# Order lists with batch 0 ahead, and cross-attention scores on 32 rows

## The chip, the cores and the metric

One core of a Trainium2 chip runs the kernel. The metric is the device time of one execution in microseconds (us). PE is TensorE, DVE is VectorE, ACT is ScalarE, POOL is GpSimd, SP is SyncE. An engine works through its own list of instructions in order, and waits at each for semaphores that other engines raise.

## The reference

Two transformer layers run one after the other on `x` of 2 batches x 512 tokens x 128 channels, 16 heads of 8 channels, with a context of 77 tokens. Layer norm, modulation and gates stand around each block.

```
layer 0:  qkv = mod(ln(x)) @ W_qkv;  x += gate * (softmax(q k^T / sqrt 8) v @ W_proj)   # all 512 tokens
          qc = ln(x) @ W_qc;  x += softmax(qc kc^T / sqrt 8) vc @ W_cproj                # 77 keys
          x += gate * (gelu(mod(ln(x)) @ W_mlp1) @ W_mlp2)
layer 1:  x += gate * (window attention: windows of 64 tokens, shifted by 32)
          x += gate * cross-attention: per query the 16 largest of 77 scores, softmax over them, times v
          x += gate * ((silu(a) * b) @ w_m2),  a, b = halves of mod(ln(x)) @ w_m1
```

## The kernel before

All is in fp32 but the self-attention of layer 0 (three bf16 parts). Tokens lie on partitions in 4 tiles of 128 per batch. PSUM has six rooms: W0 and W1 of two banks, X0, X1, M0, M1 of one. `rooms_in_turns` (L95) runs through the program once and writes down which result takes which room in which turn; `open_room` (L232) makes PE wait until the room's last result was read. Each engine's order is written out by hand in its block.

- Layer 0's self-attention ends at 163 us. It isn't touched.
- Cross-attention of either layer goes in 16 halves `e` (`HALVES`): batch, tile of 128 tokens, 8 of 16 heads. On PE a half has `cross_scores` (L1552: two products of 4 heads x 77 = 308 columns, with the keys in a block-diagonal `kblk` so that all 128 rows are used), `cross_turn` (L1565, eight transposes of the weights) and, every second half, `cross_pv` (L1575) and `pv_turn` (L1536).
- In layer 0 a half is a maximum (L1262) and a subtraction (L1267) on DVE, an exponential (L885) and two copies of turned weights (L919) on ACT.
- In layer 1 ACT copies the scores (L891); DVE finds the first 8 of each head (MAX8, L1281), strikes them out (MATCH_REPLACE8, L1284), finds the next 8 (L1288) and strikes them out (L1291), 32 instructions of 77 columns per half; POOL subtracts the maximum (L721), ACT takes two exponentials (L904, L909) and POOL multiplies them (L725).
- Window attention goes in 8 units (batch, tile). `window_qk` (L1348) and `v` project; `window_maxima` (L1588) has two groups of 32 small products per unit, each reduced by DVE (L1163); the maxima go back as a row by DMA. `window` (L1606) has, per unit, the scores (S), the products with V (V) and the turn (T). Both batches are projected first, then all units follow in the order of `WINDOWS` (L52).
- Order of the blocks: cross-attention of layer 0 for both batches, its MLP for batch 0 and then 1, window attention, cross-attention of layer 1 for both batches, its MLP for batch 0 and then 1. `ARRIVE` (L63) says at which half the projection, layer norm and query of batch 1 come.
- `project` (L1380) and `mlp_out` (L1392) write `out`, `residual` (L1049) adds it to `x`, `ln_stats` (L955), POOL's `rstd` (L607) and `ln_norm` (L971) follow, then `ln_T` (L1331) and ACT's copy to `hT`.

Of the kernel before, what the change touches and what calls it, by code (L numbers as in the profile page):

```python
# [40 lines left out]
G = 4  # L41
# [10 lines left out]
WINDOWS = "S0 S1 V0 S2 V1 T0 S3 V2 T1 S4 V3 T2 S5 V4 T3 oT S6 V5 T4 out S7 T5 lnT qc".split()  # L52
WINDOWS_LATE = {0: ("V6",), 1: ("V7", "T6"), 2: ("T7",)}
# [9 lines left out]
ARRIVE = ({"oT": -1, "out": 1, "lnT": 3, "qc": 5}, {"oT": 2, "out": 3, "lnT": 4, "qc": 5})  # L63
# [30 lines left out]

def rooms_in_turns():  # L95
# [21 lines left out]
    for layer in range(2):  # L117
        if layer == 1:
            for b in range(B):
                if b:  # L120
                    use("M", "lnT", 3, 1)
                for c in range(NQ):
                    use("M", "qkv", 1, b, "q", c)
                    use("X", "qkv", 1, b, "k", c)
                use("M", "qkv", 1, b, "v")
                for i in range(NT):
                    for half in range(2):
                        use("W", "maxw", b, i, half)
                use("M1", "mT", 1, b)
        if layer == 0:  # L130
            for t in range(STEPS):
                j = t - LOOK - 1
                for q in range(NT):
                    if t < HEADS:
                        use("Y", "max", t, q)
                    if q < 2 and 0 <= t - LOOK < UNITS:
                        use("W", "sT", 0, t - LOOK, q)
                    if q == 1 and t % G == 0 and 1 <= t // G <= B * NG:
                        use("Y", "mT", 0, t // G - 1)
                    if q == 2 and j % NT == 0 and 0 <= j < UNITS:  # L140
                        use("M0", "pv", 0, j // NT)
                for item in EARLY.get(t, ()):
                    for kind, key in EARLY_ROOMS[item]:
                        use(kind, *key)
                if j > 0 and j % NT == 0:
                    use("Y", "pvT", 0, j // NT - 1)
                for at, key in ((T_OUT, ("oT", 0, 0)), (T_OUT + 2, ("out", 0, 0)),
                                (T_OUT + 5, ("lnT", 1, 0)), (T_OUT + 7, ("qc", 0, 0))):
                    if t == at:
                        use("Y", *key)  # L150
        else:
            def window(item):
                u = int(item[1]) if item[1:].isdigit() else None
                if u is None:
                    use("X", *{"oT": ("oT", 2, 0), "out": ("out", 3, 0), "lnT": ("lnT", 4, 0), "qc": ("qc", 1, 0)}[item])
                elif item[0] == "S":
                    for half in range(2):
                        use("W", "sT", 1, u, half)
                else:
                    use(*(("M0", "pv") if item[0] == "V" else ("M1", "pvT")), 1, u)  # L160

            for item in WINDOWS:
                window(item)
        for e in range(-1, HALVES + 3):
            if e + 1 < HALVES:
                use("W", "sc", layer, e + 1)
            if layer == 1:
                for item in WINDOWS_LATE.get(e, ()):
                    window(item)
            if 1 <= e <= HALVES:  # L170
                for part in range(2):
                    use("X", "pT", layer, e - 1, part)
            if e % 2 == 0 and 1 <= e // 2 <= B * NT:
                use("M0", "pvc", layer, e // 2 - 1)
            if e % 2 == 0 and e >= 4:
                use("M1", "pvcT", layer, e // 2 - 2)
            for at, room, key in ((ARRIVE[layer]["oT"], "M1", ("oT", 2 * layer, 1)),
                                  (ARRIVE[layer]["out"], "M1", ("out", 3 * layer, 1)),
                                  (ARRIVE[layer]["lnT"], "W" if layer else "M1", ("lnT", 3 * layer + 1, 1)),
                                  (ARRIVE[layer]["qc"], "W" if layer else "M1", ("qc", layer, 1)),  # L180
                                  (11, "M1", ("oT", 2 * layer + 1, 0)), (13, "M1", ("out", 3 * layer + 1, 0)),
                                  (15, "M1", ("lnT", 3 * layer + 2, 0))):
                if e == at:
                    use(room, *key)
            if e > HALVES:
                for c in (0, 1) if e == HALVES + 1 else (2, 3):
                    use("X", "mlp", layer, 0, c)
                    if layer == 1:
                        use("W", "mlpb", 0, c)
        use("M", "oT", 2 * layer + 1, 1)  # L190
        use("M", "out", 3 * layer + 1, 1)
        use("M", "out", 3 * layer + 2, 0)
        use("M", "lnT", 3 * layer + 2, 1)
        for c in range(NC_):
            use("X", "mlp", layer, 1, c)
            if layer == 1:
                use("W", "mlpb", 1, c)
# [1591 lines left out]
```

## Time and profile before

| | |
|---|---|
| median of 3 runs | 461.62 us (460.95 to 465.91) |
| this profiled execution | 460.53 us, of which the span of instructions is 458.7 |
| PE busy | 374.1 us (82%) |
| DVE busy | 297.2 us (65%) |
| ACT busy | 204.3 us (45%) |
| POOL busy | 111.9 us (24%) |
| mean granted clock of PE | 0.851 |

The page's slices, 11.5 us each, in tenths (the clock row is the granted clock of PE, 9 stands for 0.9 or more):

```profile
PE   3999899999989987899888889978574566675985
...
DVE  4648556999897056666338361235989999997342
ACT  1311126666756935666432123332453555653511
POOL 5332304910010011001015100011434544444010
PEclk9965659999999999999999585566877877776999
```

Self-attention of layer 0 fills slices 1 to 14, its cross-attention and MLP 15 to 21, window attention 22 to 27, the top-16 cross-attention 28 to 36, the end 37 to 40.

### The profile page before, as it was taken

How to read it: one execution, taken by the hardware profiler on the slowest of the kernel's cores; microseconds unless marked ns; L12 is line 12 of the kernel's file. 1: busy time of each engine (PE TensorE's matmuls, PEld its weight loads, DVE VectorE, ACT ScalarE, POOL GpSimd, SP SyncE). 2: the span in 40 equal slices, each digit the busy share in tenths (PEclk: the TensorE clock that was granted, in tenths of full speed). 3: DMA queues.
4: the chain of work that ended last, by engine and by line, in shares of the span. 5: the costliest groups of instructions: out<-in, count | busy, mean ns of one | idle time of the engine just before them, and what ended most of it. 6: DMA issues, size and time to landing. Idle time of an engine off the chain costs nothing.

```text
span 458.7 us, 8982 instructions
## 1 busy us (share of the span) xinstructions
PE 374.1 (82%) x3317; PEld 210.5 (46%) x3317; DVE 297.2 (65%) x1279; ACT 204.3 (45%) x303; POOL 111.9 (24%) x130
## 2 busy tenths in 40 slices
PE   3999899999989987899888889978574566675985
PEld 2325412223333155677655567754353344454454
DVE  4648556999897056666338361235989999997342
ACT  1311126666756935666432123332453555653511
POOL 5332304910010011001015100011434544444010
PEclk9965659999999999999999585566877877776999
DMA  7544625110000000000000000000000000000000
GB/s 201 37 157 120 186 59 156 53 55 2 3 1 2 0 1 1 1 2 1 1 1 2 4 1 7 3 3 1 1 1 1 2 2 1 1 1 1 1 24 24
DMA packets 13247, 12.88 MB, mean 28 GB/s; under 512 B 2373, under 2 KB 11681, under 8 KB 13203
## 3 DMA queue, kind: packets, MB, share of 16 engines
q1 hardware_dynamic: 13007, 12.28, 10.3%
q8 instruction: 27, 0.44, 0.4%
q14 instruction: 17, 0.14, 0.1%
q0 software_dynamic: 160, 0.01, 0.0%
q10 hardware_dynamic: 36, 0.01, 0.0%
HBM read 9.41 MB, written 2.63 MB: 26 GB/s over the span
## 4 chain that ended last, share of the span: by engine, by line
PE 57%; DVE 29%; ACT 7%; issue 5%; POOL 1%; DMA 1%; SPq 0%; ACTq 0%; DVEq 0%; POOLq 0%
PE psum L1491 6%; PE psum L1561 5%; PE psum L1529 5%; DVE left L1284 4%; DVE left L1291 4%; PE psum L1514 4%; DVE mx L1210 4%; PE psum L1355 3%; PE psum L1660 3%; DVE top L1281 3%; DVE top L1288 3%; PE psum L1508 3%; PE psum L1485 2%; PE psum L1544 2%; PE psum L1628 2%
## 5 line engine op out<-in xcount | busy, mean ns | idle before, releaser
L1210 DVE TENSOR_REDUCE mx<-psum 128x1 f32<-128x512 f32 x128 | 81.4, 684 | 26.4 <-PE psum L1491 18.0
L803 ACT ACTIVATE big<-psum 128x1024 f32<-128x1024 f32 x64 | 62.5, 1022 | 46.1 <-PE psum L1514 25.2
L607 POOL TENSOR_TENSOR rstd<-vareps,minus_half 128x4 f32<-128x4 f32 x12 | 12.2, 1020 | 178.8 <-DVE vareps L969 178.7
L1561 PE MATMUL psum<-kblk,qf 128*128 128x308 f32 x128 | 46.0, 490 | 1.1 <-DVE qf L1157 0.8
L1572 PE MATMUL psum<-ident,pr 128*77 128x128 f32 x256 | 38.3, 299 | 10.5 <-POOL pr L725 10.5
L1491 PE MATMUL psum<-KS,QS 72*128 72x512 bf16 x112 | 43.0, 417 | 3.0 <-DVE mx L1210 2.3
L1572 PEld LDWEIGHTS psum<-ident,pr 128*77 128x77 f32 x256 | 34.4, 167 | 18.4 <-POOL pr L725 13.9
L725 POOL TENSOR_TENSOR pr<-pr,early 128x616 f32<-128x616 f32 x16 | 23.9, 1493 | 55.8 <-ACT early L909 37.8
L1529 PE MATMUL psum<-big,V 128*9 128x512 f32 x256 | 34.3, 609 | 0.5 <-ACT big L803 0.5
L1584 PE MATMUL psum<-QS,vc 77*9 77x128 f32 x256 | 13.9, 342 | 24.1 <-ACT QS L919 24.0
L1514 PE MATMUL psum<-QS,KS 75*128 75x512 bf16 x112 | 32.8, 379 | 0.4
L1561 PEld LDWEIGHTS psum<-kblk,qf 128*128 128x128 f32 x128 | 26.4, 227 | 11.1 <-issue 4.3
L1491 PEld LDWEIGHTS psum<-KS,QS 72*128 72x128 bf16 x112 | 9.9, 101 | 45.9 <-issue 25.2
L1040 DVE RECIPROCAL rden<-psum 128x16 f32<-128x16 f32 x24 | 6.1, 254 | 34.8 <-PE psum L1544 34.8
L1291 DVE MATCH_REPLACE8 left<-top,left 128x77 f32<-128x77 f32 x128 | 27.0, 234 | 0.0
L1284 DVE MATCH_REPLACE8 left<-top,gates 128x77 f32<-128x77 f32 x128 | 26.9, 230 | 0.0
L1052 DVE TENSOR_TENSOR x<-psum,x 128x512 f32<-128x512 f32 x12 | 8.3, 691 | 25.5 <-PE psum L1388 15.4
L756 ACT ACTIVATE hT<-psum,mod 128x512 f32<-128x512 f32 x10 | 7.8, 776 | 36.5 <-PE psum L1335 36.5
L919 ACT ACTIVATE big<-psum 77x512 f32<-77x512 f32 x32 | 17.1, 586 | 11.3 <-PE psum L1572 11.2
L1281 DVE MAX8 top<-gates 128x8 f32<-128x77 f32 x128 | 19.5, 228 | 3.8 <-ACT gates L891 3.8
L721 POOL TENSOR_TENSOR early<-gates,top 128x616 f32<-128x616 f32 x16 | 19.6, 1225 | 8.6 <-DVE top L1281 8.2
L891 ACT ACTIVATE gates<-psum 128x616 f32<-128x616 f32 x16 | 10.9, 682 | 22.3 <-PE psum L1561 22.2
(202 smaller groups left out, 687.3 us busy)
## 6 DMA issues: line engine op xcount, KB each, us to landing
QS<-scr_q SPq DMA_DIRECT2D x7, 288.0 KB
KS<-scr_k SPq DMA_DIRECT2D x7, 288.0 KB
scr_q<-qp SPq DMA_DIRECT2D x2, 384.0 KB, 2.9
scr_k<-kp SPq DMA_DIRECT2D x2, 384.0 KB, 3.6
gates<-scr_g SPq DMA_DIRECT2D x2, 320.0 KB, 4.1
early<-in_L_xcond_w_ada_dram SPq DMA_DIRECT2D x1, 576.0 KB, 5.1
scr_k<-kp SPq DMA_DIRECT2D x2, 256.0 KB, 4.3
wmlp<-in_L_xcond_W_mlp_dram SPq DMA_DIRECT2D x2, 256.0 KB, 3.2
```

Source lines behind the costliest of these rows:

```text
L721: pool.tensor_tensor(diff[:, k, :].rearrange("p (h s) -> p h s", s=S), sc[:, k, :].rearrange("p (h s) -> p h s", s=S), top[:, k, :, 0:1].b ...
L725: pool.tensor_tensor(pr[:, k, :], pr[:, k, :], taken[:, k, :], ALU.mult).then_inc(s_pr, 1)
L803: freed(act.activation(pT[:, u % 2, 1024 * half:1024 * (half + 1)], ps, ACT.Exp), "sT", 0, u, half)
L1210: freed(dve.tensor_reduce(mx[:, n % 3, at:at + 1], ps, AX_X, ALU.max), "max", t, q)
L1281: dve.max(top[:, k, h, 0:8], row(sc, h)).then_inc(s_top, 1)
L1284: dve.match_replace(out=row(left, h), in_to_replace=top[:, k, h, 0:8], in_values=row(sc, h), imm_value=-BIG).then_inc(s_top, 1)
L1291: ins_ = dve.match_replace(out=row(left, h), in_to_replace=top[:, k, h, 8:16], in_values=row(left, h), imm_value=-BIG)
L1491: filled(pe.matmul(ps, QS[b][0:ROWS, h, q * P:(q + 1) * P], KS[b][0:ROWS, h, :], start=True, stop=True), "max", j, q)
L1514: last = pe.matmul(ps[:, t * N:(t + 1) * N], KS[b][0:ROWS + 3, h, kt * P:(kt + 1) * P], QS[b][0:ROWS + 3, h, :], start=True, stop=True)
L1529: last = pe.matmul(ps[QUAD * hh:QUAD * hh + DV, :], V[:, b, kt, G * g + hh, :], pT[:, j % 2, hh * N:(hh + 1) * N], start=(kt == 0), stop=( ...
L1561: last = pe.matmul(ps[:, 512 * a:512 * a + HH // 2 * S], qf[:, b, i * P:(i + 1) * P], kb[:, c0:c0 + HH // 2 * S], start=True, stop=True)
L1572: last = pe.transpose(ps[0:S, t * P:(t + 1) * P], pr[:, e % 2, S * h:S * (h + 1)], ident[:, :])
```

## The change

The hand-written loops behind layer 0's self-attention become one list of pieces per engine (`pe_order`, `dve_order`, `act_order`). The names of pieces: `sc` scores, `T` turn of weights, `C` product with the context's V, `D` its turn and division, `oT` turn of the attention's output, `outNB` output N of batch B (0 self, 1 cross, 2 MLP in layer 0; 3, 4, 5 in layer 1), `res` its residual, `statNB` and `normNB` the statistics and norm before stage N, `lnT` its transposes and copy to `hT`, `wqk` and `wv` window projections, `max` maxima, `S`, `V`, `W` scores, product and turn of a window unit (0 to 3 are batch 0, 4 to 7 batch 1). Batch 0 now goes ahead: its window projection comes before batch 1's MLP of layer 0, its cross-attention of layer 1 before the last four window units of batch 1, and its last MLP lies within the halves of batch 1.

Besides that:

- Scores of the cross-attention use the 32 rows of their four heads, and each of the two products another row group. In layer 1 they have room W0 alone; the last four window units have W1 alone.
- Window maxima and scores use 32 rows where they used 8 and 9.
- The gated MLP's second product goes two chunks at a time into a room of two banks.
- POOL's order, and where some tiles lie, follow (`kblk` per batch, `wqkF` in `V`, `pcT` of layer 0 in `QS[0]`, a buffer `oraww`).

```diff
+def cross_pieces(e, layer):
+    last = B * NT * 2
+    found = [("sc", layer, e + 1)] if e + 1 < last else []
+    turns = [("T", layer, e - 1)] if 1 <= e <= last else []
+    if e % 2 == 0 and 1 <= e // 2 <= B * NT:
+        turns.append(("C", layer, e // 2 - 1))
+    if layer == 0 and e % 2 == 0 and e >= 4:
+        turns.append(("D", layer, e // 2 - 2))
+    if layer == 1 and e % 2 and e >= 3:
+        turns.append(("D", layer, (e - 3) // 2))
+    return found, turns
+def pe_order():
+    order = []
+    with_cross0 = {-1: "oT01", 1: "out01", 3: "lnT11", 5: "qc01", 11: "oT10", 12: "out10", 14: "lnT20"}
+    mlp0 = {15: (0, 1), 16: (2, 3)}
+    for e in range(-1, HALVES + 3):
+        found, turns = cross_pieces(e, 0)
+        order += found + turns + pieces(with_cross0.get(e, ""))
+        order += [("mlp0", 0, c) for c in mlp0.get(e, ())]
+        if e == 17:
+            order += [("out", 2, 0)]
+    order += pieces("oT11 lnT30 out11") + [("wqk", 0, 0), ("wqk", 0, 1)] + pieces("lnT21")
+    order += [("wqk", 0, 2), ("wqk", 0, 3)] + [("mlp0", 1, c) for c in range(NC_)] + pieces("wv0")
+    order += [("max", 0, i, half) for i in range(NT) for half in range(2)] + pieces("out21 mT0 lnT31")
+    order += [("wqk", 1, c) for c in range(NQ)]
+    order += pieces("wv1 S0 S1 V0 max100 S2 V1 W0 max101 S3 V2 W1 max110 max111 V3 W2 max120 W3 max121 "
+                    "oT20 max130 max131 out30 mT1 lnT40 qc10")
+    ahead = {0: "S4 S5", 1: "V4 S6 V5", 2: "S7 W5 V6", 3: "W6 V7", 4: "oT21", 6: "lnT41", 10: "oT30", 12: "lnT50"}
+    behind = {1: "W4", 3: "W7", 4: "out31", 6: "qc11", 10: "out40", 15: "out50"}
+    for e in range(-1, HALVES + 1):
+        found, turns = cross_pieces(e, 1)
+        order += found + pieces(ahead.get(e, "")) + turns + pieces(behind.get(e, ""))
+        order += [("mlp1", 0, e - 12)] if e in (12, 13) else []
+    order += [("D", 1, B * NT - 1)] + pieces("oT31 out41 lnT51") + [("mlp1", 1, 0), ("mlp1", 1, 1)] + pieces("out51")
+def dve_order():
+    with_cross0 = {1: "res01 stat11", 2: "norm11", 5: "qc01", 13: "res10 stat20", 14: "norm20", 18: "res20 stat30"}
...
+    order += pieces("norm30 res11 stat21 q00 norm21 q01 q02 q03 v0")
+    order += [("max", 0, i, half) for i in range(NT) for half in range(2)] + pieces("res21 stat31 mT0 norm31")
+    order += pieces("q10 q11 q12 q13 v1 max100 W0 max101 W1 max110 max111 W2 max120 W3 max121 max130 max131 "
+                    "res30 stat40 mT1 norm40 qc10")
+    inside = {2: "W5", 3: "W6", 5: "res31 stat41", 11: "res40 stat50", 13: "gate00 gate01"}
+    behind = {1: "W4", 3: "W7", 5: "norm41", 6: "qc11", 11: "norm50", 14: "gate02 gate03", 15: "res50"}
+    for e in range(HALVES):
+        order += [("first8", e)] + pieces(inside.get(e, "")) + [("next8", e)]
+        if e % 2 and e >= 3:
+            order.append(("D", 1, (e - 3) // 2))
+        order += pieces(behind.get(e, ""))
+    order += [("D", 1, B * NT - 1)] + pieces("res41 stat51 norm51 gate10 gate11 gate12 gate13 res51")
+def act_order():
+    with_cross0 = {0: "oT01", 4: "lnT11", 12: "oT10", 15: "lnT20"}
+    mlp0 = {15: (0, 1), 16: (2, 3)}
...
+    order += pieces("S0 S1 V0 S2 V1 S3 V2 V3 oT20 lnT40")
+    ahead = {0: "S4 S5", 1: "V4 S6 V5", 2: "S7 V6", 13: "mlp100 mlp101"}
+    behind = {3: "V7", 4: "oT21", 6: "lnT41", 10: "oT30", 12: "lnT50", 14: "mlp102 mlp103"}
+    for e in range(HALVES + 2):
+        if e < HALVES:
+            order.append(("copy", e))
+        if 0 <= e - 2 < HALVES:
+            order.append(("T", 1, e - 2))
+        order += pieces(ahead.get(e, ""))
+        if 1 <= e <= HALVES:
+            order.append(("diff", e - 1))
+        if e >= 3 and e % 2:
+            order.append(("C", 1, (e - 3) // 2))
+        if 1 <= e <= HALVES:
+            order.append(("left", e - 1))
+        order += pieces(behind.get(e, ""))
...
+        if kind == "sc":
+            use("W" if args[0] == 0 else "W0", *piece)
...
+        elif kind == "S":
+            for half in range(2):
+                use("W" if args[0] < NT else "W1", "sT", 1, args[0], half)
...
                 for a in range(2):
                     c0 = S * (HH * (e % 2) + HH // 2 * a)
-                    last = pe.matmul(ps[:, 512 * a:512 * a + HH // 2 * S], qf[:, b, i * P:(i + 1) * P],
-                                     kb[:, c0:c0 + HH // 2 * S], start=True, stop=True)
+                    r0 = QUAD * (2 * (e % 2) + a)
+                    last = pe.matmul(ps[:, 512 * a:512 * a + HH // 2 * S], qf[r0:r0 + QUAD, b, i * P:(i + 1) * P],
+                                     kb[r0:r0 + QUAD, c0:c0 + HH // 2 * S], start=True, stop=True)
...
+                            last = pe.matmul(ps[w * WIN:(w + 1) * WIN, j, c * WIN:(c + 1) * WIN],
+                                             QF[q0:q0 + QUAD, b, c, t0:t0 + WIN], KF[q0:q0 + QUAD, b, c, t0:t0 + WIN],
+                                             start=True, stop=True)
...
+                ps = open_room(pe, "mlpb", b, pair)
+                for j in range(2):
+                    w0 = HID + (2 * pair + j) * P
+                    last = pe.matmul(ps[:, N * j:N * (j + 1)], w[:, w0:w0 + P], hT[:, b, :], start=True, stop=True)
+                filled(last, "mlpb", b, pair)
```

## Rows read from the trace of the kernel before

**Rows 1.** Stretches: start:end, length, busy PE, PEld, DVE, ACT, POOL, granted clock, DMA, GB/s.

```profile
53.40:64.50 11.10, 11.10 (x24) 2.64 (x24) 4.41 (x7) 3.07 (x3) 0.00 (x0) 0.50 0.16 46
163.20:222.90 59.70, 54.02 (x526) 39.65 (x527) 36.90 (x79) 36.30 (x64) 5.92 (x5) 1.00 0.01 2
...
268.40:277.00 8.60, 6.35 (x261) 5.49 (x261) 6.72 (x10) 1.08 (x1) 0.00 (x0) 0.73 0.01 4
277.00:301.50 24.50, 23.31 (x669) 19.09 (x669) 3.34 (x9) 10.64 (x21) 0.00 (x0) 0.50 0.02 5
...
316.10:418.50 102.40, 64.79 (x533) 44.72 (x531) 99.09 (x807) 50.59 (x85) 44.72 (x34) 0.80 0.00 1
```

**Rows 2.** Chain that ended last, layer 0's cross-attention: start, us, engine, tile, line.

```profile
189.76 1.04 PE psum L1561 x4
...
192.90 0.60 ACT pr L885
...
193.87 0.61 ACT big L919
...
195.51 1.04 PE psum L1561 x4
```

**Rows 3.** The same chain, products of 512 columns: 32 rows twice, then 128 rows.

```profile
59.98 2.01 PE psum L1508 x4
...
67.86 1.06 PE psum L1508 x4
...
219.20 1.72 PE psum L1660 x4
```

**Rows 4.** The same chain, MLP output and a batch's window projections.

```profile
236.50 3.81 PE psum L1400 x32
...
258.61 8.84 PE psum L1355 x16
```

**Rows 5.** Timeline of PE and ACT, window stage: start, us, engine, line, operation.

```profile
272.06 3.67 PE L1599 MATMUL psum<-KS 8*64 8x64 f32 x128 [0.22 <-DVE mxw L1163]
...
276.96 1.65 PE L1628 MATMUL psum<-KS 9*64 9x64 f32 x64
...
278.16 1.10 ACT L812 ACTIVATE big<-psum 128x512 f32<-128x512 f32 x2 [8.68 <-PE psum L1628]
...
280.38 1.06 PE L1641 MATMUL psum<-big,QS 128*18 128x64 f32 x32
...
301.52 1.79 PE L1388 MATMUL psum<-wso,res 128*128 128x128 f32 x8
```

**Rows 6.** The chain again: MAX8 of the first and the second half.

```profile
316.06 1.21 DVE top L1281 x8
...
321.73 1.12 DVE top L1281 x8
```

**Rows 7.** Timeline, top-16 stage and tail.

```profile
322.65 1.49 POOL L725 TENSOR_TENSOR pr<-pr,early 128x616 f32<-128x616 f32 x1 [4.00 <-ACT early L909]
...
324.19 1.99 PE L1572 MATMUL psum<-ident,pr 128*77 128x128 f32 x8 [4.15 <-POOL pr L725]
...
327.18 0.34 DVE L1174 RECIPROCAL rdenw<-psum 64x32 f32<-64x32 f32 x1
...
341.85 0.69 DVE L1052 TENSOR_TENSOR x<-psum,x 128x512 f32<-128x512 f32 x1 [2.05 <-PE psum L1388]
...
344.00 1.22 DVE L1281 MAX8 top<-gates 128x8 f32<-128x77 f32 x8
...
349.56 1.12 DVE L974 TENSOR_SCALAR xhat<-x,mv,rstd 128x128 f32<-128x128 f32 x4
...
418.53 0.25 DVE L1040 RECIPROCAL rden<-psum 128x16 f32<-128x16 f32 x1
...
437.06 0.69 DVE L1052 TENSOR_TENSOR x<-psum,x 128x512 f32<-128x512 f32 x1 [1.55 <-PE psum L1388]
...
445.21 0.75 DVE L1184 SCALAR_TENSOR_TENSOR big<-psum,cols,qf 128x512 f32<-128x512 f32 x1 [3.08 <-PE psum L1664]
```

More of the change, by code:

```diff
@@ L116, in rooms_in_turns @@
     use("M1", "qkv", 0, 0, "k")
[L117 to L150, printed above, removed]
-        else:
[L152 to L197, printed above, removed]
-        if layer == 0:
-            use("W", "lnT", 3, 0)
-        use("M", "out", 3 * layer + 2, 1)
@@ new lines, in _ @@
+            for b in range(B):
+                if b == 0:
+                    ln_out(0, 0)
+                    wait_read(act, "vecs")
+                    rows_k_out()
+                k_out(b)
+                q_first(b)
+                if b == 0:
+                    ln_out(0, 1)
+                k_mid(b)
+                q_mid(b)
+            ps = read_room(act, "ctxT")
+            freed(act.activation(ctxT[:, :, :], ps[:, 0:2 * B * S].rearrange("p (l n) -> p l n", l=2), ACT.Copy), "ctxT")
@@ new lines, in turned_weights_out @@
+            def turned_weights_out(layer, f):
+                s = f // 2
+                if s >= 2 and f % 2 == 0:
+                    wait_full(act, "pvc", layer, s - 2)
+                for part in range(2):
+                    ps = read_room(act, "pT", layer, f, part)
+                    h0 = HH * (f % 2) + 4 * part
+                    freed(act.activation(pcT[:, s % 2, h0:h0 + 4, :], ps[0:S, :].rearrange("p (h t) -> p h t", t=P),
+                                         ACT.Copy), "pT", layer, f, part)
@@ new lines, in hidden @@
+            def hidden(layer, b, c):
+                ps = read_room(act, "mlp", layer, b, c)
+                if layer == 0:
+                    v = VECS["L0_b_mlp1"] + c
+                    ins_ = act.activation(gT[:, b, c, :], ps, ACT.Gelu_apprx_tanh, bias=cols[:, v:v + 1])
+                else:
+                    v = VECS["L1_b_m1"] + c
+                    if c == 2:
+                        wait_read(act, "mlpb", b, 0)
+                    ins_ = act.activation(sa[b][c % 2], ps, ACT.Silu, bias=cols[:, v:v + 1])
+                freed(ins_, "mlp", layer, b, c)
@@ new lines, in first_eight @@
+            def first_eight(e):
+                k, base = e % 2, 3 * HH * e
+                wait_read(dve, "sc", 1, e)
+                if e >= 2:
+                    dve.wait_ge(s_ex, HALVES + 2 * (e - 1))
+                    dve.wait_ge(s_diff, e - 1)
+                row = lambda t, h: t[:, k, S * h:S * (h + 1)]
+                for h in range(HH):
+                    dve.max(top[:, k, h, 0:8], row(sc, h)).then_inc(s_top, 1)
+                for h in range(HH):
+                    dve.wait_ge(s_top, base + h + 1)
+                    dve.match_replace(out=row(left, h), in_to_replace=top[:, k, h, 0:8],
+                                      in_values=row(sc, h), imm_value=-BIG).then_inc(s_top, 1)
@@ new lines, in next_eight @@
+            def next_eight(e):
+                k, base = e % 2, 3 * HH * e
+                row = lambda t, h: t[:, k, S * h:S * (h + 1)]
+                for h in range(HH):
+                    dve.wait_ge(s_top, base + HH + h + 1)
+                    dve.max(top[:, k, h, 8:16], row(left, h)).then_inc(s_top, 1)
+                for h in range(HH):
+                    dve.wait_ge(s_top, base + 2 * HH + h + 1)
+                    ins_ = dve.match_replace(out=row(left, h), in_to_replace=top[:, k, h, 8:16],
+                                             in_values=row(left, h), imm_value=-BIG)
+                ins_.then_inc(s_left, 1)
@@ new lines, in window_pv @@
+            def window_pv(u):
+                b, i = steps[u]
+                ps = open_room(pe, "pv", 1, u)
+                if i == 0:
+                    wait_read(pe, "qkv", 1, b, "v")
+                for half in range(2):
+                    wait_read(pe, "sT", 1, u, half)
+                for h in range(H):
+                    c, j = divmod(h, NQ)
+                    p0 = HALF * j + WIN * c
+                    last = pe.matmul(ps[QUAD * j:QUAD * j + 2 * DV, c * WIN:(c + 1) * WIN],
+                                     VW[:, b, i, h, :, :].rearrange("p w e -> p (w e)"),
+                                     pT[:, u % 2, p0:p0 + WIN], start=True, stop=True)
+                filled(last, "pv", 1, u)
```

894 lines of the change are left out of this document (423 added, 471 removed).

## The prediction

> **What bounds the kernel now.** I read the page's 40 slices first, then the busy times by stretch, the chain of work that ended last, and the timeline. Up to 163 us (self-attention of layer 0) nothing changes. What follows has four parts, and each has another limit [rows 1]. In layer 0's cross-attention (163.2 to 222.9) PE is busy 54.0 of 59.7 us at a granted clock of 1.00. In the window attention (277.0 to 301.5) PE is busy 23.3 of 24.5 us, but at 0.50, the lower of its two levels (1.2 GHz of 2.4). In the top-16 cross-attention (316.1 to 418.5) DVE is busy 99.1 of 102.4 us: every microsecond for which DVE waits there is lost. The last 40.2 us are a chain of layer norm, MLP and output with every engine partly idle.
>
> The chain shows what the page's busy PE hides. Of two halves of layer 0's cross-attention (5.75 us from score to score) only one score product is on the chain; the rest is ACT, with copies of turned weights and an exponential, and then PE again [rows 2].
>
> **The scores on row groups.** A score (`sc`) is two products of 308 columns over all 128 rows: 1.04 us at full clock [rows 2], twice that at half. After, each product has 32 rows and its own row group. The nearest rows are layer 0's first head group, whose two 32-row products of 512 columns on two row groups took 1.06 us at full clock and 2.01 at half, where two full-height products of 512 columns took 1.72 at full clock [rows 3]. Scaled by 308/512 that is 0.64 and 1.21. Bounds: 0.52 (perfect overlap) and 1.04 (none). I take 0.68 and 1.3, close to the row and a little above it because these products alternate with full-height transposes. The Trainium skill ("TensorEngine Tiling (Array Packing)", Key Properties) says that changing the tiling mode drains TensorE, and gives no price; each of the 32 scores would pay that twice. By it the sum would move towards the bound of 1.04, where nothing is gained. The trace does not show a drain by itself: the 1.06 us lie between products of 72 rows and hold whatever such a switch costs there.
>
> On the chain 0.36 us per pair of halves is won, not 0.72: ACT's run from the copies of one half over the exponential to those of the next now ends later than the shorter PE run. Up to the thirteenth score that makes 2.4 us (0.7 in the first halves, then about 0.4 per pair, qc included).
>
> **The end of layer 0.** Batch 0 is pulled ahead, and that costs batch 1 its place. `out10` comes a step earlier, but its residual and statistics (2.2 us on DVE) still stand between two subtractions, so the gain ends there. ACT now has `lnT20` and the first two GELUs ahead of the copies of the last turn: its copies start at 217.8 (before 216.8), although everything ahead ran 2.4 us earlier. `out20` (3.8 us, the like is in [rows 4]) stands ahead of the last `D`, which ends at 226.6 (before 221.2), and DVE does `res20 stat30` before its division. Then `oT11` 0.6, `lnT30`, `out11` and the copy to `hT`: the first window projection of batch 0 starts at 232.4, where before it started at the end of `out21`, 240.3 [rows 4]. So far 7.9 us are won.
>
> **The window stage until the first MAX8.** Batch 0's projections take 6.9 us (8 of 0.86, half of the 1.72 in [rows 3]). In their middle `lnT21` waits for batch 1's norm and for `q01` to empty its PSUM room, 1.9 us. Then come four hidden products 3.5 and `v` 1.0: 246.0. The eviction of `v` and the eight maxima take 8.3, as batch 1's did (8.6 with their turn, [rows 1]): 254.3. Here the gain is lost. `out21` (3.8 at full clock, about 5 as the maxima have let the clock fall) stands behind the maxima; its residual, statistics, `rstd` and norm take 4.6, and PE has only `mT0` meanwhile; `lnT31` and the copy 2.1; batch 1's projections 8.7, as before, because they start after a pause [rows 4], and `v` 1.1: 275.2. Before, this point was at 268.4. From there on less stands ahead of `out30`: four units of scores (1.64 each), four products with V and four turns (about 1.0 each, [rows 5]), eight maxima (0.92 each), `oT20` 1.1, in all 22.8 at half clock less 0.9 for its start at full: 297.1. Before, `out30` started at 301.5. From there to the first MAX8 it took 14.5 us [rows 5, 6], now 13.6 with the shorter score: **310.7, against 316.1**.
>
> **The first four halves of the top 16.** DVE needs 5.67 us per half [rows 6]. With four window divisions (0.77 each, 0.72 to the next MAX8 in [rows 7]) and one other (0.55) the four halves take 26.3 us of DVE. But the four last window units are now threaded through them, and ACT, PE and POOL have them in a strict order. Counted from the first MAX8, at half clock:
>
> - ACT does the exponentials of S4 and S5 before score copy 1. Both units go through one PSUM room, W1, in four halves one after the other, each 1.2 until its exponential starts, 0.55, and 0.1 back [rows 5]: 7.4 us after the second score (1.3). Copy 1 ends at 9.4; DVE was done at 5.7. Wait 3.7.
> - DVE has `W4` after half 1. On PE that turn stands behind T0, T0 waits for POOL's product, that for ACT's two exponentials, and those stand behind S6 and V5: score 1.3, V4 1.0, S6 with an exponential between its halves 2.65, V5 1.0, its copy 0.55, exponentials 0.7 and 0.8, POOL 1.65, T0 2.1 (1.49 and 1.99 with their lags, [rows 7]), W4 1.0, together 12.75 and 0.2 to DVE. DVE waits from 15.1 to 22.4: 7.3.
> - `W5` inside half 2 is 1.2 late. `W6` inside half 3 is behind T1, C0 and a score: 4.3. `W7` waits for the room that the first `D` empties: 0.9.
>
> Together 17.4. At full clock the same steps give 7 (1.7, 4.0, 1.3). As the clock was 0.50 in the window stage [rows 1], I take 16: these halves end at 353.0.
>
> **The other twelve halves.** Before, they took 74.5 us (344.0 to 418.5), with five divisions, a query and one residual with statistics and norm in them, and without a wait. Another residual with statistics adds 2.15, its norm 1.1, and four gate products of 0.75, moved here from the tail, 3.0 [rows 7]: 80.8, and 1.3 for waits. ACT gets four more table loads around batch 0's SiLU; they fall in halves 13 and 14, where ACT (busy 50.6 of 102.4, [rows 1]) has over a microsecond to spare. If that goes, a score copy is late and DVE waits for it. The batch 0 MLP on PE (10.7) lies under DVE as well. End 435.1; before, the last half ended at 418.5.
>
> **The tail.** From the last MATCH_REPLACE to batch 1's residual 9.4 us (POOL's product, T, copies, C, D, division, turn, projection; before 18.5, with batch 0's MLP between, [rows 7]); from that residual to the end of the span 21.6 as before, and 0.75 because two gate products now wait for one pair of banks. 31.8, before 40.2: the gain is 8.4.
>
> **Sum.** 435.1 + 31.8 = 466.9 against a span of 458.7: 8.2 us longer. Against this profiled execution's 460.5 that is 468.7; the median of the runs shown lies 1.1 above it. I predict 469. All the rest (32 rows instead of 8 or 9 in the window products, with the same columns; POOL's order; weights in another tile) I cost at nothing. The POOL work moved lies in 36 us of PE-bound time in which POOL was nearly idle [rows 1]; without that cover it is 3 us.
>
> **Rivals.**
>
> *The clock stays up in the window stage: faster.* The window products now stream 32 rows instead of 9. If the granted clock is near 1.00 from the maxima on, the 22.8 us become 14, `out21` and the second projections save 3, the norm chain 2, and the waits of the first halves fall to 7: 22 less, 447. For it: PE was as busy there as in layer 0, and the clock fell only when the products of 8 and 9 rows began (0.73 over the maxima, then 0.50, [rows 1]). Against it: at 53 to 64 us PE was busy without a gap with 32-row products on two groups and 72-row ones, and stayed at 0.50 [rows 1]. It decides if the clock of the window stage passes about 0.8.
>
> *The waits of the first halves are the full-clock ones (7), the rest as forecast: no change,* 460. For it: the turns among these steps are full-height. Against it: PE idles between them.
>
> *The clock falls in layer 0's cross-attention: much slower.* The scores were the largest full-height work there. At half clock a pair of halves takes 9.7 us of PE (two scores 2.6, turns 3.9, C 2.2, D 1.0) instead of 5.4. Two pairs make 477, all eight 503. For it: the stretch of 32-row products at 0.50. Against it: turns and products with V make up nearly two thirds of that stage and stay as they are, and 1.00 was held through all its pauses.
>
> *The row groups do not overlap:* 0.36 lost per pair, 472, inside the forecast's own range.
>
> **How the numbers follow.** Forecast 463 to 475: 0.50. Clock up: 0.20. No change: 0.17. Clock down: 0.13. The range to be held 8 times in 10 is 447 to 482: it takes in the faster rival's time and leaves out that of a long fall of the clock. About 1% (4.6 us) is what a measurement of this kernel can tell from no change. Slower by more: 0.13 and most of the forecast's 0.50, 0.55. Faster: 0.22. Within: 0.23.
>
> **What would show it.** The first projection of the window stage near 232; the first MAX8 near 311; DVE idle before L1281 and before the window reciprocal in the first four halves, released by ACT's copy and PE's turn, 16 us in all; the last half near 435; and a tail of 32. It is wrong if the clock of the window stage is not near 0.50, if the four halves take 33 us or less, or if the second projections start before 262.

## The result, and the profile after

The changed kernel takes 500.15 us (median; 495.35 to 513.82), the kernel before 463.76 beside it: a ratio of 1.077 (95% interval 1.063 to 1.091). Slower was forecast, 469 was not: the time lies 18 us above the upper end of the range.

In some executions of these kernels the clock stays at 0.50 for longer in layer 0's self-attention, which the change doesn't touch, and all that follows is up to 20 us later; so stages are compared by their lengths, from the first maximum of layer 0's cross-attention on (at 164.9 before, 172.5 after). The profiled execution of the changed kernel took 513.8 us, 13.7 above the median, and its first maximum comes 7.6 later than before; if the median execution starts as the kernel before does, its stages are by an estimate 6 us shorter than those below. In us, from the profiled executions:

| stage | before | predicted | after | new order, scores on 128 rows |
|---|---|---|---|---|
| first maximum of layer 0's cross-attention to the first window projection | 75.3 | 67.5 | 92.8 | 75.4 |
| to the first MAX8 | 75.9 | 78.3 | 80.1 | 79.1 |
| first four halves of the top 16 | 27.9 | 42.3 | 41.4 | 43.8 |
| other twelve halves | 74.6 | 82.1 | 86.3 | 86.4 |
| tail, to the end of the span | 40.1 | 31.8 | 39.0 | 38.0 |
| sum | 293.8 | 302.0 | 339.5 | 322.7 |

So the stages of this execution are 37.5 us longer than the forecast (the median lies 31 above it): 25.3 in the first row, 1.8 and 4.2 in two others and 7.2 in the tail, less 0.9. The same stretches as in [rows 1], after (start:end, length, busy PE, PEld, DVE, ACT and POOL, granted clock, DMA, GB/s):

```profile
171.10:197.00 25.90, 21.19 (x198) 13.40 (x202) 17.30 (x35) 13.04 (x24) 7.77 (x8) 0.93 0.01 2
197.00:248.00 51.00, 47.77 (x280) 31.15 (x281) 18.47 (x40) 21.55 (x36) 4.51 (x3) 0.50 0.00 1
248.00:260.90 12.90, 9.28 (x85) 6.74 (x84) 3.11 (x14) 3.62 (x6) 0.51 (x1) 1.00 0.01 1
...
310.00:320.00 10.00, 8.35 (x366) 7.01 (x364) 3.58 (x7) 6.05 (x10) 0.00 (x0) 1.00 0.02 3
320.00:331.60 11.60, 10.03 (x313) 8.12 (x309) 5.95 (x12) 2.53 (x5) 0.00 (x0) 0.79 0.02 4
345.39:473.00 127.61, 90.22 (x877) 59.58 (x878) 107.21 (x821) 65.72 (x104) 45.35 (x35) 0.66 0.01 1
```

Before, layer 0's cross-attention ran at 1.00 throughout; here the clock is 0.50, the lower of its two levels, for 51 us on end, and PE is busy for 47.8 of them. The first window units run at 1.00, where before all ran at 0.50. PE's timeline at either clock (start, us, engine, line, operation):

```profile
174.19 0.79 PE L1624 MATMUL psum<-kblk,qf 32*128 32x308 f32 x4 [0.34 <-DVE gates L1325]
174.94 1.10 PE L1635 MATMUL psum<-ident,pr 128*77 128x128 f32 x8
...
198.56 1.40 PE L1624 MATMUL psum<-kblk,qf 32*128 32x308 f32 x4
199.88 1.99 PE L1635 MATMUL psum<-ident,pr 128*77 128x128 f32 x8
...
207.92 1.40 PE L1624 MATMUL psum<-kblk,qf 32*128 32x308 f32 x4
```

A score takes 0.75 us until the turn behind it starts at full clock and 1.32 at half, close to the 0.68 and 1.3 forecast. But 8 of the 16 scores, from 198.56 to 233.51, lie in the stretch at 0.50, and there two halves take 9.36 us (198.56 to 207.92) instead of 5.75 [rows 2]. DVE's waits in the first four halves of the top 16:

```profile
354.80 1.22 DVE L1338 MAX8 top<-gates 128x8 f32<-128x77 f32 x8 [3.75 <-ACT gates L963]
...
367.41 0.35 DVE L1254 RECIPROCAL rdenw<-psum 64x32 f32<-64x32 f32 x1 [6.95 <-PE psum L1604]
...
380.97 0.35 DVE L1254 RECIPROCAL rdenw<-psum 64x32 f32<-64x32 f32 x1 [3.70 <-PE psum L1604]
...
386.04 0.35 DVE L1254 RECIPROCAL rdenw<-psum 64x32 f32<-64x32 f32 x1 [0.72 <-PE psum L1604]
```

They are 15.1 us, at the places and by the releasers that the prediction named, where 16 were forecast (W5's 1.2 did not come).

### The profile page after: what moved, and what is told of

Its sections match the earlier page's. It is cut to its first block, busy times and chain, and to the rows that moved or that the text cites. A ratio compares the mean times of both kernels' runs of the same rounds, so it can differ in the third digit from the quotient of the medians.

```text
span 512.0 us, 9039 instructions
## 1 busy us (share of the span) xinstructions
PE 414.2 (81%) x3317; PEld 224.0 (44%) x3317; DVE 299.2 (58%) x1279; ACT 212.4 (41%) x307; POOL 111.7 (22%) x130
## 4 chain that ended last, share of the span: by engine, by line
PE 61%; DVE 21%; issue 8%; ACT 5%; POOL 3%; DMA 1%; SPq 0%; POOLq 0%; ACTq 0%; DVEq 0%
PE psum L1635 7%; PE psum L1553 6%; PE psum L1591 5%; PE psum L1624 4%; PE psum L1576 4%; PE psum L1462 3%; PE psum L1647 3%; PE psum L1570 3%; DVE mx L1279 3%; PE psum L1414 3%; DVE xhat L1055 2%; PE psum L1606 2%; PE psum L1713 2%; PE psum L1547 2%; DVE left L1341 2%
## 5 line engine op out<-in xcount | busy, mean ns | idle before, releaser
L890 ACT ACTIVATE big<-psum 128x1024 f32<-128x1024 f32 x64 | 62.6, 1022 | 52.7 <-PE psum L1576 27.5
L1635 PE MATMUL psum<-ident,pr 128*77 128x128 f32 x256 | 53.9, 377 | 20.8 <-POOL pr L816 20.5
L1635 PEld LDWEIGHTS psum<-ident,pr 128*77 128x77 f32 x256 | 44.0, 212 | 37.4 <-POOL pr L816 25.0
L989 ACT ACTIVATE QS<-psum 77x512 f32<-77x512 f32 x64 | 36.5, 590 | 53.9 <-PE psum L1635 53.9
L1553 PE MATMUL psum<-KS,QS 72*128 72x512 bf16 x112 | 45.6, 442 | 2.8 <-DVE mx L1279 2.1
L1624 PE MATMUL psum<-kblk,qf 32*128 32x308 f32 x128 | 36.0, 651 | 4.1 <-ACT gates L963 2.1
L1591 PE MATMUL psum<-big,V 128*9 128x512 f32 x256 | 36.9, 650 | 0.5 <-ACT big L890 0.5
L1576 PE MATMUL psum<-QS,KS 75*128 75x512 bf16 x112 | 34.0, 391 | 0.4
L1396 PE MATMUL psum<-ident,xhat 128*128 128x128 f32 x48 | 11.5, 384 | 27.4 <-DVE xhat L1055 25.6
L1647 PE MATMUL psum<-QS,vc 77*9 77x128 f32 x512 | 26.1, 355 | 4.2 <-ACT QS L989 4.1
L844 ACT ACTIVATE hT<-psum,mod 128x512 f32<-128x512 f32 x10 | 7.8, 776 | 50.7 <-PE psum L1396 50.7
L1396 PEld LDWEIGHTS psum<-ident,xhat 128*128 128x128 f32 x48 | 7.7, 194 | 31.6 <-issue 28.6
```

The lines of the kernel that those rows point to most:

```text
L890: freed(act.activation(pT[:, u % 2, 1024 * half:1024 * (half + 1)], ps, ACT.Exp), "sT", 0, u, half)
L989: freed(act.activation(pcT[:, s % 2, h0:h0 + 4, :], ps[0:S, :].rearrange("p (h t) -> p h t", t=P), ACT.Copy), "pT", layer, f, part)
L1553: filled(pe.matmul(ps, QS[b][0:ROWS, h, q * P:(q + 1) * P], KS[b][0:ROWS, h, :], start=True, stop=True), "max", j, q)
L1576: last = pe.matmul(ps[:, t * N:(t + 1) * N], KS[b][0:ROWS + 3, h, kt * P:(kt + 1) * P], QS[b][0:ROWS + 3, h, :], start=True, stop=True)
L1591: last = pe.matmul(ps[QUAD * hh:QUAD * hh + DV, :], V[:, b, kt, G * g + hh, :], pT[:, j % 2, hh * N:(hh + 1) * N], start=(kt == 0), stop=( ...
L1624: last = pe.matmul(ps[:, 512 * a:512 * a + HH // 2 * S], qf[r0:r0 + QUAD, b, i * P:(i + 1) * P], kb[r0:r0 + QUAD, c0:c0 + HH // 2 * S], st ...
```

## The experiments

The lengths below are those of one profiled execution each: layer 0 (first to last maximum of its cross-attention), window (to the first MAX8), top 16 (to the end of the last MATCH_REPLACE), tail. How far they can be trusted shows in the top 16 of the seven kernels in the new order that leave the window units inside it: 127.5 to 131.4. The medians hold the unequal starts as well.

| kernel | layer 0 | window | top 16 | tail | sum | median of runs | before, beside it |
|---|---|---|---|---|---|---|---|
| before | 47.5 | 103.7 | 102.6 | 40.1 | 293.8 | | 463.8 |
| after | 62.6 | 110.3 | 127.6 | 39.0 | 339.5 | 500.2 | 463.8 |
| 1 order alone | 50.8 | 103.7 | 130.2 | 37.9 | 322.7 | 488.9 | 464.5 |
| 2 scores alone | 58.1 | 102.7 | 103.6 | 40.0 | 304.4 | 480.3 | 464.5 |
| 3 after, layer 0 on 128 rows | 49.1 | 104.2 | 127.6 | 35.6 | 316.5 | 493.9 | 464.5 |
| 4 as 1, window on 8 and 9 rows | 50.8 | 110.6 | 127.9 | 36.3 | 325.6 | 490.8 | 464.5 |
| 5 before, window on 32 rows | 49.0 | 100.0 | 102.8 | 40.2 | 292.0 | 471.3 | 473.6 |
| 6 as 1, units ahead | 50.7 | 109.4 | 109.6 | 38.3 | 308.0 | 484.2 | 473.6 |
| 7 as 1, out50 behind | 50.6 | 104.5 | 131.4 | 37.7 | 324.2 | 493.1 | 473.6 |
| 8 before, scores on 32 rows, twice | 53.4 | 104.0 | 104.2 | 41.8 | 303.4 | 480.9 | 473.6 |
| 9 as 5, longer maxima | 49.0 | 106.8 | 103.0 | 41.7 | 300.5 | 465.3 | 469.6 |
| 10 as 6, gates unpaired | 50.7 | 111.4 | 111.1 | 38.1 | 311.2 | 483.2 | 469.6 |
| 11 after, scores twice | 71.1 | 109.6 | 127.7 | 38.8 | 347.2 | 504.1 | 469.6 |
| 12 as 5, more runs | 49.2 | 98.6 | 104.0 | 39.4 | 291.2 | 455.5 | 469.6 |
| 13 after, layer 0 on 64 rows | 70.9 | 109.6 | 127.5 | 39.0 | 347.1 | 508.0 | 472.2 |
| 14 before, layer 0 on 64 rows | 69.1 | 104.5 | 103.5 | 41.8 | 318.9 | 489.4 | 472.2 |

### Which part lets the clock fall (1 to 3)

```
1: after.py, cross_scores, both layers (3: in layer 0 alone)
-  qf[r0:r0 + QUAD, b, i * P:(i + 1) * P], kb[r0:r0 + QUAD, c0:c0 + HH // 2 * S]
+  qf[:, b, i * P:(i + 1) * P],            kb[:, c0:c0 + HH // 2 * S]
2: the reverse of it in before.py
```

> The changed kernel with its cross-attention scores back on all 128 rows, in both layers: the new order alone. Theory A (the 32-row scores let the granted clock fall in layer 0's cross-attention, and the order costs its own 8 us): the clock stays at 1.00 through that stage, about 60 us long, and the kernel takes 470 (466 to 475). Theory B (it is the order: the pauses of PE behind the residuals of batch 1 and 0 are where the clock falls): the clock falls in that stage again and the time stays at 492 to 500. Theory C (either alone is harmless, the two together are not): as A here.

> The kernel before with its cross-attention scores on the 32 rows of their four heads, in both layers: the new scores alone, in the old order. Theory A: the clock falls in layer 0's cross-attention, pairs of halves there take 9.4 us instead of 5.75, the stage some 20 to 30 us more, and the kernel takes 485 to 495. Theory B: the clock stays, each pair gains 0.4, and the kernel takes 460 (457 to 463). Theory C: as B.

> The changed kernel with its scores on 128 rows in layer 0 alone, on 32 rows in layer 1. Theory A: like the order alone, 470 (466 to 475), since in layer 1 DVE is the bound and a score is off its path. Theory B: 492 to 500. If instead the 32-row scores of layer 1 hold the clock down there too, and the longer halves of layer 1 come from that, this run lies 3 us or more over the order alone.

The order alone takes 488.9 us, a ratio of 1.063 (1.050 to 1.076); the scores alone 480.3 (471.2 to 482.0), layer 0 put back 493.9 (482.9 to 500.1). Windows of the order alone, then of the scores alone:

```profile
159.00:171.00 12.00, 9.06 (x80) 6.52 (x78) 9.37 (x24) 4.56 (x8) 1.98 (x2) 1.00 0.00 1
171.00:175.50 4.50, 4.50 (x22) 3.86 (x19) 2.04 (x3) 2.58 (x5) 3.53 (x6) 0.62 0.00 0
175.50:214.00 38.50, 34.84 (x366) 25.47 (x365) 24.40 (x49) 22.31 (x41) 5.94 (x4) 1.00 0.01 2
```

```profile
184.00:190.00 6.00, 5.07 (x32) 3.20 (x32) 3.77 (x7) 3.36 (x7) 1.27 (x1) 0.51 0.00 0
190.00:200.50 10.50, 9.11 (x97) 5.52 (x98) 5.78 (x9) 6.09 (x12) 0.00 (x0) 0.96 0.01 2
200.50:224.00 23.50, 23.42 (x152) 15.07 (x145) 9.72 (x17) 9.50 (x17) 0.00 (x0) 0.51 0.00 1
```

With 128 rows the clock dips for 4 us, after the pause behind batch 1's residual, and comes back; with 32 it comes back too, falls a second time after the next pause (1.3 us without work on PE; in 1, pauses of 1.15 and 1.00 did not lower it), and then stays down although PE no longer pauses. Theory A holds for the clock in all three; theory B, which had it fall in 1 and 3, falls, and so does C, by which the scores alone were harmless. The sizes of A were off: the order alone costs 29 us by the stage sums, not 8 to 11, so that 1 and 3 lie far above 466 to 475; and in 2 the stage grew by 10.6, not 20 to 30, as the clock came back at 224 (480.3 us, not 485 to 495). Taking layer 0's scores back to 128 rows saves 17 (1) and 23 us (3) of the changed kernel's 339.5 by the stages, and 11 and 6 by the medians, where the intervals of the changed kernel (1.063 to 1.091) and of 1 overlap: that the clock falls is shown; what it costs is known only as 6 to 23 us. The mean granted clock is 0.75 to 0.79 in all four executions of the changed kernel and 0.83 to 0.86 in those of 1. The median of 3 lies 5 us above that of 1, named beforehand as the sign that layer 1's 32-row scores cost time; its top 16 is no longer (127.6 against 130.2), so the stages don't bear that out.

### Height, or time (8, 11, 13, 14)

```
8, 11: in layer 0
+  for again in range(2):
       last = pe.matmul(... qf[r0:r0 + QUAD, ...], kb[r0:r0 + QUAD, ...])
13, 14: in layer 0, both products on the same 64 rows, one after the other
+  rows = slice(2 * QUAD * (e % 2), 2 * QUAD * (e % 2) + 2 * QUAD)
```

> The kernel before, with the 32-row scores in layer 0 alone and each of their products issued twice over the same columns (the second writes the same numbers again), so that PE is not idle for longer than before. Theory A (it is the height of the scores that lets the clock fall): it falls in layer 0's cross-attention as with the scores alone, for 15 us or more, and the kernel takes 475 to 490. Theory B (the scores alone left PE idle for longer, and that let it fall): the clock stays at 1.00 there but for short dips, and the kernel takes 462 to 468.

> The changed kernel with each 32-row score product of layer 0 issued twice over the same columns; all else as changed. Theory A (in the old order this kept the clock at 1.00 but for one dip, and the order does not matter to it): the clock stays at 1.00 but for a dip in layer 0's cross-attention, from the first to the last subtraction it takes 53 to 56 in place of 62.6, and the kernel takes 485 to 492, less than the changed kernel although it does more. Theory B (in the new order the pauses are longer and it falls all the same): 62 or more and 498 to 508.

> The changed kernel with layer 0's scores on 64 rows (their eight heads' and no others; both products on the same rows, so one after the other, as with 128 rows); layer 1's stay on 32. A score takes 1.04 us again, so PE is busy exactly as with 128 rows, and only the height differs. Theory A (the height of the products lets the clock stay down): after the pause behind batch 1's residual the clock stays at 0.50 for 15 us or more, or at least longer than the 3 to 5 us that every kernel with 128 rows showed. Theory B (it is the shorter score, or two products at once on two row groups): one dip of 3 to 5 us, from the first to the last subtraction 49 to 51, and a time of 483 to 494, as with layer 0 on 128 rows.

> The kernel before with layer 0's scores on 64 rows, one product after the other, 1.04 us a score. Theory A: a fall of 15 us or more in layer 0's cross-attention, as with 32 rows, and 470 to 482. Theory B: at most one dip of 3 to 5 us and the time of the kernel before within 3 us.

Windows of 8, 11 and 14, in this order:

```profile
184.00:192.00 8.00, 6.26 (x38) 4.00 (x38) 4.58 (x9) 3.83 (x7) 1.30 (x2) 0.59 0.00 0
192.00:234.00 42.00, 40.06 (x425) 27.49 (x426) 24.47 (x49) 24.74 (x46) 2.23 (x2) 1.00 0.01 2
```

```profile
188.50:202.50 14.00, 13.06 (x133) 8.12 (x133) 6.69 (x12) 6.98 (x13) 2.25 (x1) 0.99 0.01 3
202.50:252.00 49.50, 48.15 (x286) 32.84 (x285) 17.89 (x38) 16.80 (x30) 4.55 (x3) 0.50 0.00 1
```

```profile
177.00:189.00 12.00, 11.04 (x111) 6.68 (x110) 6.21 (x11) 6.37 (x12) 0.00 (x0) 1.00 0.01 2
189.00:227.00 38.00, 38.00 (x198) 25.14 (x197) 13.11 (x21) 13.28 (x23) 0.00 (x0) 0.51 0.00 1
```

And of 13:

```profile
189.00:238.00 49.00, 47.65 (x255) 31.92 (x254) 18.13 (x38) 16.73 (x29) 4.55 (x3) 0.50 0.00 1
```

The doubled scores disagree: in the old order one longer dip (theory B for the clock, though 480.9 us is in the range of A), in the new one a fall of 50 us (theory B of 11), although PE had more to do than with 128 rows; 504.1 us. The 64-row scores decide it for theory A: PE has the time of 128 rows and no two products overlap, and the clock stays at 0.50 for 38 us in the old order and about 50 in the new (489.4 us, above the 470 to 482 expected, and 508.0). So it is not the time of the products or their overlap but that they use fewer rows. What these runs don't separate is the fewer rows themselves from the change between few rows and all that comes with each such score. In all, every trace with fewer than 128 rows in layer 0 but that of 8 has a fall of 23 us or more (5 of 6); none of the ten with 128 rows has one, though eight of them show the dip. Why 8 held is open, so fewer rows make the fall likely here, not certain.

### The rows of the window products (4, 5, 12, 9)

```
4: 1 with the window products as in before.py;  5, 12: before.py with
-  QF[q0:q0 + D, ...],  KF[q0:q0 + D, ...]       # maxima; scores: DV
+  QF[q0:q0 + QUAD, ...], KF[q0:q0 + QUAD, ...]  # both
9: 5, and in the maxima
+  for again in range(2 - j):
```

> The order alone, and the window products back on 8 and 9 rows in place of 32 (same columns). Costed at nothing: within 2 us of the order alone, with a clock of 0.50 over the window stage in both. Rival: the 32 rows do hold the clock up for part of that stage, and this run is 3 to 6 us slower than the order alone.

> The kernel before, with its window products (maxima and scores of layer 1) on 32 rows in place of 8 and 9, same columns, nothing else changed. Theory A (in the runs of the order alone the clock stayed at 1.00 over the window units with 32 rows and fell to 0.50 with 8 and 9): the stretch of window units, 24.5 us at 0.50, loses 6 to 10 us and the kernel takes 452 to 457. Theory B (the order of those runs held the clock, not the rows): the clock is 0.50 there as before and the time is that of before within 2 us.

> The kernel before with its window products on 32 rows, once more with more rounds. Its trace showed 3.7 us less from the last subtraction of layer 0 to the first MAX8 and nothing more than 1.5 elsewhere. Theory A: 0.5 to 1 per cent faster than the kernel before. Theory B: no difference.

> The kernel before with window products on 32 rows (as measured already: the clock fell to 0.50 over the maxima, where PE stops between banks for DVE, and stayed there until the sixth unit), and now the products of every other group of rows in the maxima issued twice over the same columns, so that PE stops for less there; the second writes the same numbers again. Theory A (it is those stops that let the clock fall before the units): the clock is 1.00 from the first maxima to the window output, the stretch from the last subtraction of layer 0 to the first MAX8 goes from 100.0 to 92 to 96, and the kernel takes 450 to 455. Theory B (the clock falls anyway): the stretch takes 100 to 104, at most 3 more for the longer maxima.

The window units in the order alone (32 rows), then in 4 (8 and 9 rows):

```profile
284.00:302.00 18.00, 15.36 (x609) 12.85 (x609) 8.50 (x17) 6.55 (x13) 0.00 (x0) 1.00 0.02 5
```

```profile
289.00:309.00 20.00, 19.70 (x488) 16.16 (x485) 8.61 (x16) 4.13 (x8) 0.00 (x0) 0.50 0.02 3
```

With 32 rows the clock stays at 1.00 and the first MAX8 comes 6.9 us sooner; 4's top 16 and tail are 3.9 shorter, within the spread of such lengths, and the medians differ by 1.9. Costing the rows at nothing was wrong for the stage. In the old order (5) they save 3.7 us there, not the 6 to 10 of theory A: the clock falls over the maxima and comes back in mid-stage (so too in 9 and 12), which it did in none of the four kernels in the old order with 8 and 9 rows. Once more with more runs (12) that is 455.5 us, a ratio of 0.985 (0.975 to 0.995), more than the 0.5 to 1% expected; the stage sums give 1.8 (5) and 2.6 us (12), 0.4 and 0.6%. The direction is clear, the size is not. Its windows over the first and the later units:

```profile
274.00:284.00 10.00, 8.74 (x271) 6.94 (x263) 1.21 (x3) 4.17 (x8) 0.00 (x0) 0.50 0.03 7
286.00:298.00 12.00, 9.98 (x400) 8.24 (x388) 3.87 (x12) 6.37 (x14) 0.00 (x0) 1.00 0.02 5
```

Longer maxima (9) didn't hold the clock over the maxima; that stretch grew from 100.0 to 106.8, so theory A of it fell, and B's size (100 to 104) was too small. That the stops for DVE lower the clock there stays unproven.

### The waits of the first four halves (6)

```
 PE:  ... max131 - out30 mT1 lnT40 qc10          + mT1 out30 S4 S5 V4 S6 V5 lnT40 W4 S7 V6 qc10 W5
 PE:  - ahead  {0: S4 S5, 1: V4 S6 V5, 2: S7 W5 V6, 3: W6 V7}  + {0: V7 W6, 1: W7}
 DVE: + W4 and W5 around qc10; W6, W7 inside halves 0 and 1;  ACT: in the same order
```

> The order alone, with the last four window units (S4 to S7 and what follows from them) put ahead of the first half of the top 16, in both banks of PSUM rooms, into the pauses of the chain from the window output to the query; the turns W6 and W7 stay inside the first two halves. Theory A (in the order alone DVE waits 17.8 us in the first four halves because those units stand ahead of the score copies and turns): the waits go, the four halves take 25 us in place of 43.8, the first MAX8 comes 3 to 10 us later, and the kernel is 8 to 15 us shorter than the order alone. Theory B (the units cost what they cost wherever they stand): the first MAX8 comes 16 us or more later and the time is that of the order alone within 3 us.

Four halves take 24.2 us instead of 43.8, the first MAX8 comes 5.7 later, the sum of stages is 14.7 less: theory A in every stage. The medians, which hold the unequal starts, differ by 4.7 (484.2 against 488.9), less than the 8 to 15 expected. Its DVE timeline has the fourth half's first MAX8 18.1 us after the first's and no wait:

```profile
334.56 1.22 DVE L1338 MAX8 top<-gates 128x8 f32<-128x77 f32 x8 [1.41 <-ACT gates L963]
...
340.86 1.20 DVE L1338 MAX8 top<-gates 128x8 f32<-128x77 f32 x8
...
352.69 1.21 DVE L1338 MAX8 top<-gates 128x8 f32<-128x77 f32 x8
```

### The tail (7, 10)

```
7:  PE:  - behind {..., 15: out50}   + oT31 out41 out50 lnT51;   DVE: res50 behind norm51
10: 6 with 32 rows in layer 1's scores, and for batch 1  + room ("mlpb", 1, c) for each gate product
```

> The order alone, with batch 0's last product (out50) moved from ahead of the last half's turn to behind batch 1's output projection, into the pause of batch 1's norm, and its residual behind batch 1's norm on DVE. In the order alone that product stood on PE from 447.1 to 451.3, ahead of the turn of half 15, whose input was there at 449.9; so from the last MATCH_REPLACE to batch 1's residual it took 13.2 us where 9.4 had been worked out. Theory A: that stretch takes 9.4 to 11 and the kernel is 2 to 4 us shorter than the order alone. Theory B (the turn waited for POOL's product anyway, or the product now delays the MLP of batch 1): no gain.

> The new order with the window units ahead of the top 16, as measured already, and two changes more: the 32-row scores in layer 1 (layer 0 keeps 128 rows), and in batch 1's last MLP each gate product in a room of its own, so that a gate waits for its own product and not for a pair. In the order alone the last gate ended 17.2 us after batch 1's residual, where the kernel before took 14.1. Theory A (that was the pairing): the stretch from that residual to the end goes from 24.8 to 22 and the whole is 2 to 4 us shorter than with the units ahead alone. Theory B (it was the load of ACT's table and the clock of 0.50 there): 24 to 25 as before.

Both were worth little. The first fence is 1, the second 7. In 1, `out50` ran for 4.4 us ahead of the last turn, and the turn behind it ran at full clock (1.04). In 7 it was out of the way, and the whole chain ran at half:

```profile
447.07 4.39 PE L1462 MATMUL psum<-wm,big 128*128 128x128 f32 x32
...
451.30 1.04 PE L1635 MATMUL psum<-ident,pr 128*77 128x128 f32 x8
...
458.20 0.69 DVE L1132 TENSOR_TENSOR x<-psum,x 128x512 f32<-128x512 f32 x1 [2.67 <-PE psum L1447]
...
464.82 3.75 PE L1713 MATMUL psum<-hT,wm 128*128 128x512 f32 x4 [0.92 <-issue]
```

```profile
463.17 1.99 PE L1635 MATMUL psum<-ident,pr 128*77 128x128 f32 x8 [2.69 <-POOL pr L816]
...
471.48 2.05 PE L1447 MATMUL psum<-gw,res 128*128 128x128 f32 x8 [0.73 <-ACT res L915]
...
473.56 0.69 DVE L1132 TENSOR_TENSOR x<-psum,x 128x512 f32<-128x512 f32 x1 [4.05 <-PE psum L1447]
...
479.72 1.96 PE L1713 MATMUL psum<-hT,wm 128*128 128x512 f32 x4 [0.92 <-issue]
```

From the last MATCH_REPLACE to that residual it took 13.2 us in 1 and 15.4 in 7: theory B, by a cause that neither named. What 7 lost there it won back behind it: `out50` now fills the pause of batch 1's norm, the MLP's first products take 1.96 us instead of 3.75, and from the residual to the end it is 22.3 us instead of 24.8. Unpairing the gates (10) took the stretch from the residual to the end from 24.9 in 6 to 23.6, where 22 was expected; the clock is 0.50 when batch 1's MLP starts, before it was 1.00. The whole was not shorter than 6 (311.2 against 308.0 by the sums, 483.2 against 484.2 by the medians), so theory A holds for less than half of its 2.8 us.

## Why the prediction was wrong, point by point

- **The step that failed first** is the clock of layer 0's cross-attention, left at 1.00 with 0.13 on the rival that it falls. That rival's mechanism and its 9.7 us per pair (9.36 measured) came. That its price for all eight pairs (503) is near the 500.2 measured is luck: the fall took in four pairs, for which its own arithmetic gives 486, and other terms added the rest. What weighed against it, that turns and products with V make up most of the stage and that 1.00 was held through all pauses, was read from a trace in which the scores were of full height; with scores of full height the clock came back, with 32 or 64 rows it stayed down for 23 us or more in all but 8 (1 and 3 against 2, 11, 13 and 14). The fall also outlived its stage: it lasted to 248, 13 us past the last maximum (235.06). Together that is the 17 to 23 us that 1 and 3 save by the stages (11 and 6 by the medians).
- **The clock was not all.** With it at 1.00 the time would still have lain above the range: 488.9 in 1 and 493.9 in 3, against 482. The terms below, mostly waits and norms that the sum sized too small, make up the other part.
- **The scores on row groups** were priced right at both clocks. The Trainium skill ("TensorEngine Tiling (Array Packing)", Key Properties) has a change of tiling mode drain TensorE. No run here shows a drain by itself, but a score at 0.75 between full-height turns is 0.07 above the forecast and far from the 1.04 at which nothing would be won, so it did not take the gain away.
- **The end of layer 0** without the fall (1): 75.4 where 67.5 and 2.4 for the higher scores were forecast. 3.3 of the 5.5 lie between the first and last maximum, with the dip of the clock, 2.2 behind it.
- **The window stage** was 80.1 for 78.3. The clock was not 0.50 throughout, as assumed, but 1.00 over the first units (rival 1 in part), which the prediction had named as a sign that it is wrong. Yet from the end of the second projections (311.4) to the first MAX8 only 1.5 us were won (34.0 for 35.5), and ahead of that 3.3 were lost (46.1 for 42.8). The steps written down for these two ends add up to 245.7 and 275.8, not 246.0 and 275.2, and 468.7 and 1.1 to 469.8; that changes nothing.
- **The first four halves** were right: 41.4 for 42.3, and 6 showed that the place of the window units is their cause.
- **The other twelve** were 4.2 too short. In 1, whose 86.4 are the same, DVE waits for a query (1.24), a gate (1.88) and a turn (1.41) instead of the 1.3 forecast, and each of two norms takes 2.33 where 1.12 was taken [rows 7]. These are 5.6 more together, where 4.2 are missing. A product of POOL runs inside the long norms, and the trace of the kernel before had such a norm too, which the prediction passed over (1, then before):

```profile
372.34 2.33 DVE L1055 TENSOR_SCALAR xhat<-x,mv,rstd 128x128 f32<-128x128 f32 x4
...
372.86 1.48 POOL L816 TENSOR_TENSOR pr<-pr,early 128x616 f32<-128x616 f32 x1 [2.60 <-ACT early L978]
```

```profile
419.02 2.34 DVE L974 TENSOR_SCALAR xhat<-x,mv,rstd 128x128 f32<-128x128 f32 x4
...
419.53 1.49 POOL L725 TENSOR_TENSOR pr<-pr,early 128x616 f32<-128x616 f32 x1 [4.00 <-ACT early L909]
```

In all sixteen traces, from layer 0's cross-attention on, a norm takes 2.05 to 2.35 us when an operation of POOL overlaps it for 1.2 to 1.5 us, and 1.10 to 1.12 when at most 0.1 us of one does; no run was made to move the one away from the other. The old order has one such long norm, the new order three.
- **The tail** was 7.2 too short, in 1 6.2 (38.0). There the stretch to batch 1's residual was 13.2 for 9.4: POOL's last product ends 4.9 us after the last MATCH_REPLACE, since ACT copies half 14's turn ahead of the exponentials it needs, and `out50` holds the turn 1.4 more. The stretch from there was 24.8 for 22.4. With the gates unpaired it was 23.6 (10); with the clock at 1.00 in batch 1's MLP and the pairs left, 22.3 (7), so the clock alone is enough to explain it.

By the stages the fall of the clock explains about half of the 37.5, and terms of the order that were sized too small the other half (18.3 in 1: 5.5, 0.8, 1.5, 4.3 and 6.2 in the five rows).

## What to carry to other kernels

A cheaper instruction on PE may be the one that keeps its clock: before full-height products are cut to fewer rows, price the whole stage at the lower clock too, and give that case a real chance. Before a norm's price is taken from one row, look at every row of it, and at what runs beside it. Where products are low anyway, raising them to more rows with the same columns (32 for 8 and 9) cost nothing and gained 2 to 3 us by the stages (1.5% by the runs, 0.5 to 2.5). Work threaded into a stage that one engine bounds costs the waits of the strict orders around it; in the pauses of the chain ahead, the same work took a third of that (5.7 us against 17.8 of waits).

## What was unexpected of the hardware

Scores on 64 of 128 rows, of the same duration as on 128, let the granted clock fall from 1.00 to 0.50 with PE busy for 38.0 of 38.0 us. Window products on 32 rows held it at 1.00 for 18 us in the new order, where 8 and 9 rows gave 0.50; in the old order only the later units had 1.00. And with 4.4 us of full-height products ahead of a turn, the chain behind them was 2.2 us shorter than without them (13.2 against 15.4); the same products put into the pause of the next norm shortened the chain behind that by 2.5 (22.3 against 24.8).
